# The running state of a linear attention kept in three parts, so that one matmul adds a head pair's three parts of v

## The reference

```python
q, k, v = split(layernorm(x) @ w_qkv)          # 16 heads of 16
q, k = elu(rope(q) * S) + 1, elu(rope(k) * S) + 1
for t in tokens:                               # a scan
    kv += outer(k[t], v[t]); ks += k[t]        # per head: the state
    o[t] = (q[t] @ kv) / max(q[t] . ks, 1e-6)
x = x + o @ w_out
h = layernorm(x)
x = x + sum_e weights(h)[e] * (silu(h @ Wg[e]) * (h @ Wu[e])) @ Wd[e]
```

## Time and profile before

| what | value |
|---|---|
| median of three runs | 799.52 us (798.75 to 800.13) |
| the profiled execution | 799.23 us, of which 797.3 are the span of the trace |
| TensorE busy | 754.6 us, 95% |
| VectorE, ScalarE, GpSimd busy | 605.1, 465.7 and 483.2 us: 76%, 58%, 61% |
| a step in the steady part, TensorE's start of L397 to the next | 22.5 us, in a router tile 24.0 us |

### The profile page before, as it was taken

The page is one execution under the profiler, slowest core; times in us unless marked ns, Lnnn a source line. Parts: engine busy times, 40 slices in busy tenths (PEclk is TensorE's granted clock), DMA queues, the critical chain, the costliest instruction groups (busy, mean ns, idle before and its releaser), DMA issues.

```text
span 797.3 us, 18061 instructions
## 1 busy us (share of the span) xinstructions
PE 754.6 (95%) x6660; PEld 647.6 (81%) x6660; DVE 605.1 (76%) x1597; ACT 465.7 (58%) x886; POOL 483.2 (61%) x537
## 2 busy tenths in 40 slices
PE   5475899999999999999999999999999999999998
PEld 3364688888888888888888888888888888888887
DVE  6788797878877797778878797887877788756344
ACT  3664666666666565666665566666656665634222
POOL 3695678765666666556667565575675656653322
PEclk9776899999999999999999999999999999999999
DMA  4544134122210221121111221210211121100000
GB/s 141 129 102 108 41 86 93 41 43 62 47 26 16 44 67 41 42 43 42 38 30 41 43 68 41 41 39 7 66 42 41 41 54 28 28 1 28 1 1 27
DMA packets 97319, 38.27 MB, mean 48 GB/s; under 512 B 74192, under 2 KB 96976, under 8 KB 97232
## 3 DMA queue, kind: packets, MB, share of 16 engines
q1 hardware_dynamic: 90704, 30.83, 17.5%
q10 hardware_dynamic: 6528, 6.29, 2.7%
HBM read 16.13 MB, written 4.19 MB: 25 GB/s over the span
## 4 chain that ended last, share of the span: by engine, by line
PE 88%; DVE 5%; ACT 2%; issue 2%; POOL 2%; DMA 0%; DVEq 0%; ACTq 0%; SPq 0%; POOLq 0%
PE y L475 22%; PE gate L441 21%; PE up L441 21%; PE front L301 6%; PE front L302 3%; PE back L353 3%; PE back L397 3%; PE up L372 2%; PE up L409 1%; PE front L324 1%; PE front L422 1%; PE back L341 1%; PE back L384 1%; POOL a_lo L1188 1%; PE back L324 1%
## 5 line engine op out<-in xcount | busy, mean ns | idle before, releaser
L1217 POOL TENSOR_TENSOR h_lo<-work,h_hi 128x512 fp32r<-128x512 f32 x126 | 163.2, 1296 | 59.2 <-ACT h_hi L677 59.2
L1188 POOL TENSOR_TENSOR a_lo<-am,a_hi 128x512 f16<-128x512 f32 x120 | 144.8, 1208 | 52.5 <-ACT a_hi L604 49.9
L475 PE MATMUL y<-wd_hi,h_hi 128*128 128x256 f32 x504 | 145.8, 289 | 0.0
L475 PE MATMUL y<-wd_lo,h_hi 128*128 128x256 f32 x504 | 140.5, 279 | 0.0
L475 PE MATMUL y<-wd_hi,h_lo 128*128 128x256 f32 x504 | 140.2, 278 | 0.0
L1061 DVE TENSOR_TENSOR work<-work,up 128x512 f32<-128x512 f32 x128 | 87.0, 680 | 61.9 <-PE up L441 61.6
L677 ACT ACTIVATE h_hi<-work 128x512 fp32r<-128x512 f32 x126 | 79.4, 630 | 58.3 <-DVE work L1061 36.4
L1077 DVE SCALAR_TENSOR_TENSOR xa<-y,wo,xa 128x256 f32<-128x256 f32 x252 | 111.9, 470 | 1.9 <-PE y L475 1.9
L475 PEld LDWEIGHTS y<-wd_hi,h_hi 128*128 128x128 f32 x504 | 94.7, 188 | 4.1
L475 PEld LDWEIGHTS y<-wd_lo,h_hi 128*128 128x128 f32 x504 | 94.9, 188 | 2.8
L475 PEld LDWEIGHTS y<-wd_hi,h_lo 128*128 128x128 f32 x504 | 95.0, 189 | 0.0
(11 more groups left out here) (220 smaller groups left out, 1738.4 us busy)
## 6 DMA issues: line engine op xcount, KB each, us to landing
xr<-xT SPq DMA_DIRECT2D x32, 128.0 KB, 2.6
xa<-x SPq DMA_DIRECT2D x32, 128.0 KB, 2.8
out<-xa SPq DMA_DIRECT2D x32, 128.0 KB, 1.7
xa<-Wg ACTq DMA_DIRECT2D x8, 256.0 KB, 3.1
work<-Wd ACTq DMA_DIRECT2D x8, 256.0 KB, 3.0
work<-Wu ACTq DMA_DIRECT2D x8, 256.0 KB, 2.8
work<-w_qkv SPq DMA_DIRECT2D x2, 384.0 KB, 3.4
qT<-q_st SPq DMA_TRANSPOSE x32, 3.2
```

The source lines that it names most:

```text
L475: m = pe.matmul(y_bank(n, t), h_at(hi, n)[:, t * P:(t + 1) * P], wd_p[wi][:, u // KI, u % KI, :], start=(n % KI == 0 and (t % 2 == 0 or n ...
L1188: pool.tensor_tensor(a_p[1][:, heads(r), :], am_place(g, r).rearrange("p (h n) -> p h n", h=4), a_p[0][:, heads(r), :], ALU.subtract).then ...
L1217: pool.tensor_tensor(h_at(1, n), hb[:, n % 2, :], h_at(0, n).bitcast(F32), ALU.subtract).then_inc(s_hlo, 1)
```

## The change

From tile 8 on (`PARTS = 8`; until then `stage` is in use) `state` makes one matmul for a pair of heads instead of three: all three parts of v at once, 2 x 51 = 102 columns, side by side. Eight pairs need 816 columns, so the first five (`NPU`) go to bank U where `state` stood, and the last three to R1, at the end of `av`'s products with the scores and ahead of `from_state`. The running sum is kept three times, in `st_p` (128 x 8 x 3 x 17, in `stage`). VectorE adds bank U to it (`st_add`, two instructions of 64 x 255) and bank R1 (`st_add_r1`, two of 64 x 153, behind `norm(c)`). GpSimd sums the three running sums into `st_s` by two instructions (`st_sum`, ahead of `v_rest(a)`), from which `s1` and `st_rest` go on as before. At tile 7 `st_parts` fills `st_p`, once. The new waits: `scores` and `s1` wait for the new steps, `st_add` for `st_sum` of the tile before.

```diff
@@ scores @@
+                if g > PARTS:
+                    w.wait_ge(s_ssr, 2 * (g - PARTS))
@@ TensorE @@
+            def state_parts(g, bank, first, last, done):
+
+                if bank is R1:
+                    w.wait_ge(s_v, tiles(g + 1))
+                for p in range(first, last):
+                    m = pe.matmul(bank[:, (p - first) * 2 * WV:(p - first + 1) * 2 * WV],
+                                  k_st[:, g % 2, 2 * p:2 * p + 2, :, :].rearrange("p h c d -> p (h c d)"),
+                                  vx[:, g % 2, 2 * p:2 * p + 2, :, :].rearrange("p h s d -> p (h s d)"),
+                                  start=(p == first), stop=(p == last - 1), skip_group_check=True)
+                m.then_inc(done, 1)
@@ av, ahead of from_state(False, True) @@
+                if g >= PARTS:
+                    state_parts(g, R1, NPU, NP, s_stater)
@@ state @@
+                if g >= PARTS:
+                    state_parts(g, U, 0, NPU, s_state)
+                    return
@@ s1 on ScalarE @@
+                if g >= PARTS:
+                    w.wait_ge(s_sum, g - PARTS + 1)
@@ VectorE @@
+            def parts_add(bank, first, last, done):
+
+                new = bank[:, 0:(last - first) * 2 * WV].rearrange("p (q h s d) -> p q h s d", q=last - first, h=2, s=3)
+                for hh in range(2):
+                    rows = slice(64 * hh, 64 * hh + 64)
+                    v.scalar_tensor_tensor(out=st_p[rows, first:last, :, :], in0=new[rows, :, hh, :, :], scalar=ASCALE,
+                                           in1=st_p[rows, first:last, :, :], op0=ALU.mult, op1=ALU.add).then_inc(done, 1)
@@ st_add @@
+                if g >= PARTS:
+                    w.wait_ge(s_stp, 2)
+                    w.wait_ge(s_sum, g - PARTS)
+                    parts_add(U, 0, NPU, s_ss)
+                    return
@@ VectorE @@
+            def st_parts(g):
+
+                if g != PARTS - 1:
+                    return
+                for n in range(SLABS - NSL, SLABS):
+                    w.wait_ge(*slab_lo_done(n))
+                w.wait_ge(s_ss, 2 * PARTS)
+                v.memset(st_p[:, :, 1:3, :], 0.0).then_inc(s_stp, 1)
+                v.tensor_copy(st_p[:, :, 0, :], st_s[:, :, :]).then_inc(s_stp, 1)
+
+            def st_add_r1(g):
+                if not live(g) or g < PARTS:
+                    return
+                w.wait_ge(s_stp, 2)
+                w.wait_ge(s_sum, g - PARTS)
+                w.wait_ge(s_stater, g - PARTS + 1)
+                parts_add(R1, NPU, NP, s_ssr)
-                route_first(router); norm(c); route_second(router); q_lo(a); k_lo(a); o_lo(c); h_up(n + 1)
+                route_first(router); norm(c); st_add_r1(c); route_second(router); st_parts(c); q_lo(a); k_lo(a); o_lo(c); h_up(n + 1)
@@ GpSimd @@
+            def st_sum(g):
+
+                if not live(g) or g < PARTS:
+                    return
+                w.wait_ge(s_ss, 2 * g + 2)
+                w.wait_ge(s_ssr, 2 * (g - PARTS) + 2)
+                w.wait_ge(s_s1, g)
+                w.wait_ge(s_sr, g)
+                pool.tensor_tensor(st_s[:, :, :], st_p[:, :, 0, :], st_p[:, :, 1, :], ALU.add).then_inc(s_sum1, 1)
+                w.wait_ge(s_sum1, g - PARTS + 1)
+                pool.tensor_tensor(st_s[:, :, :], st_s[:, :, :], st_p[:, :, 2, :], ALU.add).then_inc(s_sum, 1)
-                slab_lo(slab(s, 1)); v_rest(a); h_lo(n); h_lo(n + 1); slab_lo(slab(s, 2)); rstd2_pow(c); st_rest(c)
+                slab_lo(slab(s, 1)); st_sum(c); v_rest(a); h_lo(n); h_lo(n + 1); slab_lo(slab(s, 2)); rstd2_pow(c); st_rest(c)
```

More of the change, by code:

```diff
@@ L45 @@
 LAST = UNITS * NB - 4
+PARTS = 8
+NPU = 5
 def bcast(ap, axis, n):
@@ L145, in build @@
         hb, stage = work[:, 0:2, :], work[:, 2:4, :]
+        st_p = stage[:, 0, 0:NP * WV].rearrange("p (q s d) -> p q s d", q=NP, s=3)
         h_p = [sb(f"h_{s}", [P, 2, B], F32R) for s in ("hi", "lo")]
@@ L171, in build @@
              "slab_hi", "slab_lo"))
-        (s_qkv, s_qk, s_av, s_state, s_oT, s_proj, s_x2T, s_lgrows, s_logit, s_gate, s_up, s_down, s_last) = (
+        (s_qkv, s_qk, s_av, s_state, s_oT, s_proj, s_x2T, s_lgrows, s_logit, s_gate, s_up, s_down, s_last, s_stater) = (
             sem(n) for n in ("qkv", "scores", "av", "state", "o_T", "proj", "x2_T", "logit_rows", "logit", "gate", "up",
-                             "down", "down_last"))
+                             "down", "down_last", "state_r1"))
         (s_xhi, s_qkc, s_v, s_exp, s_qhi, s_khi, s_v1, s_v2, s_ahi, s_s1, s_s2, s_ohi, s_lgc, s_th, s_e1, s_fb,
@@ L182, in build @@
         (s_slab_lov, s_xlo, s_bn, s_mv, s_ve, s_tcos, s_cos, s_rope, s_phi, s_qlo, s_klo, s_amask, s_o, s_ss, s_den, s_rec, s_norm, s_olo, s_x1,
-         s_bn2, s_mv2, s_ve2, s_x2n, s_x2lo, s_h, s_acc, s_hlov) = (sem(n) for n in (
+         s_bn2, s_mv2, s_ve2, s_x2n, s_x2lo, s_h, s_acc, s_hlov, s_stp, s_ssr) = (sem(n) for n in (
              "slab_lo_v", "x_lo", "bn", "mv", "ve", "tcos", "cos", "rope", "phi", "q_lo", "k_lo", "masked", "o", "ss", "den", "rec", "norm",
-             "o_lo", "x1", "bn2", "mv2", "ve2", "x2n", "x2_lo", "h", "acc", "h_lo_v"))
+             "o_lo", "x1", "bn2", "mv2", "ve2", "x2n", "x2_lo", "h", "acc", "h_lo_v", "state_parts", "ss_r1"))
         ROUTE = ("sum", "inh", "off", "zone", "dist", "zone2", "m", "eq", "w0", "c", "ws", "ix", "no", "s1", "nd",
@@ L188, in build @@
         s_route = sem("router_step")
-        s_rstd1, s_sin, s_vr, s_v3, s_alo, s_sr, s_s3, s_rstd2, s_hlo = (sem(n) for n in (
-            "rstd1", "sin", "vr", "v3", "a_lo", "sr", "s3", "rstd2", "h_lo"))
+        s_rstd1, s_sin, s_vr, s_v3, s_alo, s_sr, s_s3, s_rstd2, s_hlo, s_sum1, s_sum = (sem(n) for n in (
+            "rstd1", "sin", "vr", "v3", "a_lo", "sr", "s3", "rstd2", "h_lo", "st_sum1", "st_sum"))
         def routed(b, step):
```

## The result

The changed kernel took 804.4 us, the median of five runs (803.24 to 805.39), beside 799.52 for the kernel before, again over five runs (798.48 to 800.13). The ratio of the two was measured as 1.0055, with a 95% interval of 1.0044 to 1.0067; the two medians alone give 1.0061. It is slower, as forecast, by 4.4 us (by the ratio) to 4.9 (by the medians) where 2.4 were forecast. The span of the profiled execution is 801.2 us, 3.9 more than before.

The account below looks back on a forecast made before the run. The chain to ox_lo, which TensorE's projection weight load awaits, was taken as the bound. Ordinary tiles 17 x -0.10 = -1.7, tile 31 -0.2, router tiles 6 x 0.72 = +4.3: +2.4 on 799.52 makes 801.9 us, range 795.5 to 804.0.

Parts of the forecast that it names:

- The bound: Projection's weight load on TensorE waits for VectorE's ox_lo, which has no room to be later in ordinary or router tiles.
- TensorE's part: State matmuls: eight of 102 columns at 48 ns replace 24 of 34 columns, 0.23 us off TensorE a tile.
- the third rival: A 102-column state matmul costs 77 ns, so eight take as long as 24 now: 804.9 us, chance 0.06.
- St_add's part: VectorE's addition of bank U: U ready 0.36 us earlier, additions 0.25 longer, so rope 0.10 earlier after the added wait.
- the second rival: VectorE's 64-row additions overlap as others do, rope 0.32 us earlier: 793.0 to 795.5 us, chance 0.15.
- The router tiles: Six tiles meeting a router step: q_lo and ox_lo 0.72 us late each, +4.3 us in all.
- The exclusion: In route_second, GpSimd's second sum stops VectorE's L1010 until about 373.35: q_lo 0.72 us late, instead of 0.26 without it.
- The room: Slack on VectorE ahead of q_lo in a router tile, taken as 0.33 us.
- The first rival: VectorE's router instructions in route_second slip in between GpSimd's sums, q_lo only 0.26 us late: 799.2 us, chance 0.27.
- Rope's lead: VectorE's rope starts 0.10 us earlier because bank U is ready sooner.
- the wait of the three R1 matmuls for v_copy: On TensorE, bank R1's three pairs come up after 321.3, v_copy is done at 320.23: costs nothing.
- the 0.2 us expected of tile 31: Tile 31 has no q_lo ahead of its ox_lo, so it was given a full gain of 0.2 us.

Follow-up runs that it names:

- second: Changed kernel with GpSimd's st_sum behind h_lo(n + 1) and VectorE's st_add_r1 behind h_up(n + 1): 801.43 us, 1.0014 to the kernel before.
- fifth: Changed kernel with st_sum behind h_lo(n + 1), st_add_r1 behind h_up(n + 1) and the R1 matmuls behind from_state: 800.79 us, 1.0010 to the kernel before.
- sixth experiments: Changed kernel with st_sum, st_add_r1 and the R1 matmuls moved back, and three pairs in bank U, five in R1: 803.13 us, 1.0038 to the kernel before.
- the first: Changed kernel with only GpSimd's st_sum moved behind h_lo(n + 1): 802.79 us, 1.0033 to the kernel before.
- the tenth experiment: Kernel before plus two VectorE additions of 64x153 between norm(c) and route_second, scratch inside an existing tile so no tensor moves: 802.62 us, 1.0024.

## Why the prediction was right, and where it was off

**The bound** was right. The weight load of the projection follows ox_lo by 0.05 us in every tile from 8 to 30, and a router tile's time moved with q_lo's start wherever that was late: 24.87 us at 6.94, 24.48 at 6.56, 24.36 at 6.46, with TensorE's work the same in the first two. Once the chain was short enough other waits took over in router tiles (second, fifth and sixth experiments), and in ordinary ones TensorE's saving came through: 22.26 us with three pairs in bank U.

**TensorE's part** was right: 48 ns a matmul, interpolated between 25 and 117, measured 47 to 50. That rejects the third rival (77 ns). The Trainium skill ("TensorE: Matmul & The Clock Gate", section "Back-to-back issue gap") has 81 ns for 128 columns in a stream of weight loads and matmuls, which is no guide to this stream; the same section's figure for an isolated matmul, N / 2.4 + 2.5 ns, gives an estimate of 45 for 102 columns and is near.

**St_add's part** was right in the lengths (421 ns in the mean for 255 columns, 0.42 predicted; 0.91 to rope, 0.90 predicted), which rejects the second rival; the fifth matmul ended 0.36 earlier, as predicted, but the addition began only 0.30 earlier; it starts 0.21 behind that matmul's end, where it had been 0.14, and the chain shows 0.05 of VectorE's queue (L69, a wait) in it. For the added wait I had allowed 0.01. So rope came 0.05 earlier, not 0.10, an ordinary tile gained 0.06, and a tile behind a router tile 0.01. Together that is 0.7 us where 1.7 had been predicted: 1.0 us of the error.

**The router tiles** hold the rest. Predicted was q_lo 0.72 late, measured 0.96 (6.94 against 5.98 us behind the first state matmul). By terms: st_add_r1 0.69, as predicted. The exclusion 0.39 (0.17 by L1059 and 0.22 by L1064), where I had 0.46, from L1064 alone; that this term is near is partly luck, for L1059, which I had left running in the forecast, was stopped too. The room 0.22, not 0.33: I had VectorE free 0.10 behind L1010's start, and the first and the tenth experiment show that q_lo can follow by 0.21 at the earliest. The first rival is out: both instructions were stopped in all six tiles. Rope's lead 0.05, not 0.10. And 0.15 that the prediction lacks: o_sum starts 0.75 behind rope instead of 0.61, because av ends late, and loses 0.01 more. I had put the wait of the three R1 matmuls for v_copy at nothing, from an ordinary tile, where v_copy ends at 320.23. In a router tile ScalarE loads a table and does a router function (L684) ahead of v_copy. ScalarE's and TensorE's timelines, tile 16, changed kernel:

```profile
366.94 1.28 ACT L684 ACT_TABLE_LOAD   x1
368.24 0.23 ACT L684 ACTIVATE router<-router 128x32 f32<-128x32 f32 x1
368.37 0.46 ACT L578 ACTIVATE vs<-front,rstd 128x256 f32<-128x256 f32 x1
...
368.89 0.31 PE L338 MATMUL front<-vx,k_st 128*128 128x102 bf16 x3 [0.32 <-ACT vs L578]
```

Two steps failed in the router tiles, then: that wait was put at nothing after a look at one kind of tile only, and the room was read 0.11 too large. Together, 0.69 + 0.39 + 0.15 - 0.05 - 0.22 of room = 0.96. Of these 0.96, 0.90 reach the tile's length; the projection's first matmul used to start 0.10 behind its weight load, under the last gate matmul, and now starts with it.

**The sum**: the tiles' lengths give 5.4 less 0.7, or 4.7, where 4.3 less 1.7 had been predicted, and the 0.2 us expected of tile 31 did not come. So of the 2.3 us that the sum was short, 1.1 are the router tiles, 1.0 the ordinary ones and 0.2 tile 31. The direction and its reason, ox_lo in the router tiles, were right; the size was half of the measured one. By the ratio the time is 803.9, just inside the range; the median lies 0.4 us above the range's end.

## What to carry to other kernels

Before work is taken off the busiest engine, look for a weight load, or any first instruction of a block, that already starts right behind another engine's result: there the room is zero, and a cheaper matmul whose result costs more to add up gives back little of what it saves (0.06 of 0.22 us here). Instructions added ahead of that result cost their length less the room. Read every added wait and every added instruction in each kind of iteration, not in the usual one; the tile of the router had 0.22 us of room where the ordinary one had 1.24. And a change that fails in the rare kind can be kept for the common one: that gave 0.9977 here, and 0.9949 with the pairs and steps also moved.

## What the runs showed of the hardware

VectorE's small instructions with two inputs in SBUF, scalar_tensor_tensor among them, when they start beside a running GpSimd instruction, end only 0.04 to 0.05 us behind it: in the median they went from 192 to 364 ns, from 182 to 399, and from 192 to 1170. L1062, with one input, keeps its 0.19 us beside the second sum. This is the lock of the Trainium skill ("SBUF — State Buffer", section "SBUF: two separate sides"), and the traces agree with it.

A tensor that nothing uses made the kernel 0.7% slower; all that it does is move those behind it. The matmuls of the experts show a part of where; TensorE's groups from 300 to 600 us, kernel before, then with the unused tensor:

```profile
L441 PE MATMUL gate<-x_hi,wg_lo 128*128 128x512 f32 x104 | 32.3, 391 | 0.0
```

```profile
L442 PE MATMUL gate<-x_hi,wg_lo 128*128 128x512 f32 x104 | 32.7, 395 | 0.0
```

The six such groups are 2 to 4 ns longer a matmul. With 48 of them a tile that is 0.1 to 0.2 us, about what the tiles grew by (from 22.5 to between 22.67 and 22.78). Which tensor's place does it, and why, stays open: no run moved one alone. An added scratch tile can thus hide or fake an effect of this size, and a control with the tensor alone is worth its run.
